# A transformer layer on eight cores: residual loads moved to ScalarE's queue, the cast cut in quarters, the output projection started 14 steps earlier

## The reference

```python
# attention: x [sq*b, 2048], 16 heads of 128
mixed = x @ Wqkv.T                       # q, k, v of each head
attn = softmax(einsum('gqd,gkd->gqk', q, k) / sqrt(128))
ctx = einsum('gqk,gkd->gqd', attn, v)
out = ctx @ Wproj.T + bproj
h1 = layernorm(x + out)
# FFN: weights are 4-bit codes times a scale per group of 128
gate, up = split(h1 @ w_gu.T)            # 5632 each
y = (silu(gate) * up) @ w_down.T
y = y / sqrt(mean(y*y) + 1e-6)
return layernorm(h1 + y)
```

## Time and profile before

| what | us |
|---|---|
| median of 3 runs | 4144.91 |
| the profiled execution, its own time | 4153.74 |
| its span, slowest core (core 2) | 4152.0 |
| spans of the eight cores | 4127.6 to 4152.0 |
| busy: PE | 4060.1 (98%) |
| busy: ACT | 1400.2 (34%) |
| busy: DVE | 948.6 (23%) |
| busy: POOL | 286.4 (7%) |

### The profile page before, as it was taken

How to read it: one execution, slowest core, us unless ns; L and a number is a source line. 1 busy time by engine, 2 the same in 40 slices (tenths; PEclk the granted TensorE clock), 3 DMA queues, 4 the chain that set the end, 5 groups by cost and what they waited for, 6 DMA issues and landing times.

```text
span 4152.0 us, 66120 instructions; the slowest of 8 cores (4127.6 to 4152.0 us)
## 1 busy us (share of the span) xinstructions
PE 4060.1 (98%) x26491; PEld 2296.5 (55%) x26881; DVE 948.6 (23%) x1433; ACT 1400.2 (34%) x1610; POOL 286.4 (7%) x434
## 2 busy tenths in 40 slices
PE   7999999999999999999999999999999999999998
PEld 4666666666666766666554444444444444444443
DVE  0054452222222223220234100022100300022124
ACT  1355555555555555557642100000000000000001
POOL 1100000000000000000223000000000000000000
PEclk9999999999999999999999999999999999999999
DMA  9777776465655655656459545447444654446433
GB/s 146 130 172 169 178 165 126 107 137 121 124 119 118 140 104 120 135 119 111 110 157 261 191 167 199 159 155 231 152 157 152 201 189 152 157 164 216 162 127 123
DMA packets 251041, 635.65 MB, mean 153 GB/s; under 512 B 115184, under 2 KB 137712, under 8 KB 212720
## 3 DMA queue, kind: packets, MB, share of 16 engines
q1 hardware_dynamic: 202496, 426.29, 31.6%
q0 software_dynamic: 45792, 196.10, 25.5%
q10 hardware_dynamic: 2448, 8.91, 0.5%
HBM read 643.83 MB, written 119.54 MB: 184 GB/s over the span
## 4 chain that ended last, share of the span: by engine, by line
PE 93%; SPq 2%; DMA 2%; issue 1%; ACT 1%; DVE 0%; POOL 0%; ACTq 0%; DVEq 0%; POOLq 0%
PE pJ L283 16%; PE pC L339 11%; PE pJ L269 11%; PE pS L320 10%; PE pS L412 7%; PE pS L393 7%; PE pS L389 7%; PE pC L389 4%; PE pJ L393 3%; PE pC L393 3%; PE pJ L389 3%; PE pJ L361 3%; PE pC L412 3%; PE pJ L412 3%; SPq L1118 2%
## 5 line engine op out<-in xcount | busy, mean ns | idle before, releaser
L496 ACT ACTIVATE P<-pS 128x1024 bf16<-128x1024 f32 x1024 | 1027.8, 1026 | 356.8 <-PE pS L320 342.6
L283 PE MATMUL pJ<-x,wq 128*128 128x512 bf16 x2984 | 756.9, 381 | 28.5 <-DMA x<-xc 23.8
L339 PEld LDWEIGHTS pC<-V,P 128*128 128x128 bf16 x8192 | 549.8, 98 | 168.0 <-issue 11.3
L339 PE MATMUL pC<-V,P 128*128 128x129 bf16 x8192 | 634.0, 220 | 3.6 <-DVE ctxg L613 3.1
L320 PE MATMUL pS<-Q,K 128*128 128x512 bf16 x1829 | 561.7, 379 | 18.9 <-ACT P L496 7.5
L269 PE MATMUL pJ<-wq,x 128*128 128x256 bf16 x4096 | 514.8, 273 | 0.4
L283 PEld LDWEIGHTS pJ<-x,wq 128*128 128x128 bf16 x3072 | 301.0, 98 | 381.9 <-issue 33.4
L269 PEld LDWEIGHTS pJ<-wq,x 128*128 128x128 bf16 x4096 | 400.7, 98 | 134.8
L609 DVE RECIPROCAL rcp<-pC 128x4 f32<-128x4 f32 x64 | 11.7, 183 | 1477.9 <-PE pC L339 1477.9
L393 PE MATMUL pS<-h1T,wgu 128*128 128x512 bf16 x1408 | 318.3, 379 | 0.0
L389 PE MATMUL pS<-h1T,wgu 128*128 128x512 bf16 x1408 | 318.3, 379 | 0.0
(11 more groups left out here) (107 smaller groups left out, 2647.8 us busy)
## 6 DMA issues: line engine op xcount, KB each, us to landing
wgu<-wgu_scr SPq DMA_DIRECT2D x176, 1024.0 KB, 4.9
x<-xc POOLq DMA_DIRECT2D x256, 512.0 KB, 12.4
wd<-wdn_scr SPq DMA_DIRECT2D x174, 512.0 KB, 3.5
wgu_scr<-bits SPq DMA_DIRECT2D x44, 1024.0 KB, 5.1
wdn_scr<-bits SPq DMA_DIRECT2D x44, 512.0 KB, 4.6
xr<-xrows SPq DMA_DIRECT2D x16, 1024.0 KB, 7.1
h_scr<-h1f POOLq DMA_DIRECT2D x16, 1024.0 KB, 7.1
res<-h_scr POOLq DMA_DIRECT2D x16, 1024.0 KB, 8.9
```

The source lines that it names most:

```text
L283: mm = t.matmul(out, M.wq[:, pair, part, hc, h * 128:(h + 1) * 128], x[:, hc, :], start=(hc == 0), stop=(hc == HC - 1))
L339: mm = t.matmul(M.pC[:, o:o + 129], M.P[n % 3][:, h * 512 + qt * 128:h * 512 + (qt + 1) * 128], M.V[s % 2][:, 2 * p + h, l, :], start=(p = ...
L496: a.activation(out=M.P[n % 3][:], in_=M.pS[n % 2][:], func=AF.Exp, bias=0.0, scale=NORM).then_inc(S.exp_done, 1)
```

## The change

Four things are changed.

1. `OC_FIRST` goes from 60 to 46: the output projection's matmuls begin at step 46 of slot 7.
2. The loads of `xr` for tiles 2 to 15 leave SP's queue. ACT issues them, each right behind the store of the `h1b` tile two before it. The first two stay on SP.
3. The cast of a tile to bf16 is cut into four instructions of 512 columns. In slot 7 one quarter stands behind each exponential; in the tail the four stand together. Every quarter waits for `h1_done` of the tile.
4. In the FFN, the four transposed loads of the next chunk stand behind operations 8, 15, 22 and 29 of the current chunk, one each. The first four context loads are placed at step 31 instead of 34, behind the same store.

```diff
-OC_FIRST = 60
+OC_FIRST = 46
+H1T_OPS = (8, 15, 22, 29)
...
-def act_h1_cast(a, S, M, tile):
+def act_h1_cast(a, S, M, k):
+    tile, ut = divmod(k, 4)
+    cols = slice(512 * ut, 512 * (ut + 1))
     a.wait_ge(S.h1_done, tile + 1)
     if tile >= 2:
         a.wait_ge(S.h1b_stored[tile % 2], 16 * (tile // 2))
-    a.copy(out=M.h1b[tile % 2][:].rearrange("t (u j p) -> t u j p", u=4, j=4),
-           in_=M.h1f[tile % 2][:].rearrange("t (u p j) -> t u j p", u=4, j=4)
-           ).then_inc(S.h1b_done, 1)
+    cast = a.copy(out=M.h1b[tile % 2][:, cols].rearrange("t (j p) -> t j p", j=4),
+                  in_=M.h1f[tile % 2][:, cols].rearrange("t (p j) -> t j p", j=4))
+    if ut < 3:
+        return
+    cast.then_inc(S.h1b_done, 1)
     a.wait_ge(S.h1b_done, tile + 1)
     a.dma_start(out=M.d_h1b[tile * 128:(tile + 1) * 128, :],
                 in_=M.h1b[tile % 2][:]).then_inc(S.h1b_stored[tile % 2], 16)
+    if tile + 2 < TILES:
+        a.wait_ge(S.oc_evac, 4 * (tile + 1))
+        a.dma_start(out=M.xr[tile % 2][:], in_=M.d_xrows[(tile + 2) * 128:(tile + 3) * 128, :]
+                    ).then_inc(S.xr_in[tile % 2], 16)
...
-        if n >= (SLOTS - 1) * STEPS and 4 * (tile + 1) <= oc_groups_done(n % STEPS - 5):
-            act_h1_cast(a, S, M, tile)
-            tile += 1
-    while tile < TILES:
-        act_h1_cast(a, S, M, tile)
-        tile += 1
+        if n >= (SLOTS - 1) * STEPS and 4 * (k // 4 + 1) <= oc_groups_done(n % STEPS - 5):
+            act_h1_cast(a, S, M, k)
+            k += 1
+    for k in range(k, 4 * TILES):
+        act_h1_cast(a, S, M, k)
...
-        if i == 34:
+        if i == 31:
...
-        sp_xr_load(y, S, M, xr + 2)
-        xr += 1
...
-            if op == 10 and ch + 1 < FCH:
-                sp_h1t_load(y, S, M, ch + 1, range(4))
+            if op in H1T_OPS and ch + 1 < FCH:
+                tt = H1T_OPS.index(op)
+                sp_h1t_load(y, S, M, ch + 1, range(tt, tt + 1))
```

More of the change, by code:

```diff
@@ L549, in act_program @@
         g += 1
-    tile = 0
+    k = 0
     for n in range(SLOTS * STEPS):
@@ L1101, in sp_ctx_load @@
                           ).then_inc(S.ctxt_in[tile % CTXT_RING], 16)
[L1104 to L1108, removed]
 def sp_h1t_load(y, S, M, ch, tiles):
@@ L1153, in sp_program @@
     y.wait_ge(S.pv_done, (SLOTS - 1) * STEPS)
-    sp_xr_load(y, S, M, 0)
-    sp_xr_load(y, S, M, 1)
-    xr = ctxt = 0
+    for tile in range(2):
+        y.dma_start(out=M.xr[tile][:],
+                    in_=M.d_xrows[tile * 128:(tile + 1) * 128, :]).then_inc(S.xr_in[tile], 16)
+    done = ctxt = 0
     for i in range(STEPS):
@@ L1164, in sp_program @@
                 ctxt += 1
-        if 4 * (xr + 1) <= oc_groups_done(i - 2):
-            sp_xr_load(y, S, M, xr + 2)
-            xr += 1
-        while ctxt - CTXT_RING < xr and 32 * (ctxt // 4 + 1) <= i:
+        if 4 * (done + 1) <= oc_groups_done(i - 2):
+            done += 1
+        while ctxt - CTXT_RING < done and 32 * (ctxt // 4 + 1) <= i:
             sp_ctx_load(y, S, M, ctxt)
@@ L1173, in sp_program @@
         y.wait_ge(S.ctx_stored[j], 16 * (SLOTS * QBLOCKS // 2))
-    while xr + 2 < TILES:
-        if xr == TILES - 5:
+    for tile in range(done, TILES - 2):
+        if tile == TILES - 5:
             sp_wgu_load(y, S, M, 0)
             sp_wgu_load(y, S, M, 1)
-        if xr >= TILES - 4:
-            sp_h1t_load(y, S, M, 0, range(2 * (xr - TILES + 4), 2 * (xr - TILES + 4) + 2))
-        while ctxt < TILES and ctxt - CTXT_RING <= xr:
+        if tile >= TILES - 4:
+            tt = 2 * (tile - TILES + 4)
+            sp_h1t_load(y, S, M, 0, range(tt, tt + 2))
+        while ctxt < TILES and ctxt - CTXT_RING <= tile:
             sp_ctx_load(y, S, M, ctxt)
             ctxt += 1
-        sp_xr_load(y, S, M, xr + 2)
-        xr += 1
     sp_wgu_load(y, S, M, 2)
```

## The result

The changed kernel is slower. Its time is 4181.70 and 4183.79 us, against 4142 to 4147 before; the ratio is 1.0092, 95% interval 1.0062 to 1.0121. Runs in which the cores of a die showed a lower granted clock (two here, 4637 and 4725 us, and one of the kernel before) are left out of every time and ratio. I had forecast 4166, with 4148 to 4190.

What follows compares the result with a forecast made beforehand. PE, busy 98% of the span, was taken as the bound. Core 0: 4139.4 + 13.4 + 2.7 - 5 + 21 - 7.4 = 4164, plus 1.7 us outside the span: 4166, range 4148 to 4190.

Steps and rivals of the forecast that it cites:

- The loop through ACT, the load, POOL and DVE: Projection's tail: each `h1f` waits on the previous one through cast, store, residual load, bias and deviation; 18.3 us a lap.
- L: Time for a residual load issued by ACT to land; taken as 6.5 us, between rows of 5.3 and 9.7.
- The tail's start: Zero point of the tail's sum, read as 2139.83 before the change, with the last exponential ending five us ahead.
- The crowding of the last two loads: Tail's end: four transposed `h1T` loads on SP run beside the last two residual loads, adding 2 us each.
- The waits and the clock: Tail: PE waits for the addition at eight tiles, 3 to 6 us each.
- The early start: Projection from step 46: a gain of 1.7 us alone, 2.7 us waiting for the first context; about +1 together.
- The quarters: Cast cut in four: 4.1 us for four in a row; PE's waits beside the exponentials shrink, -5 us.
- The spread `h1T` loads: FFN: PE's weight waits and slow matmuls behind them go, 18 us on core 2 and 7.4 on core 0.
- the loads land on time: Rival for the tail: the loop does not bind, 19 us less there on core 0, time 4126; 7%.
- a light loop: Rival for the tail: L 5.3, lap 17.1, nothing added at the end, time 4151; 15%.
- a heavy loop: Rival for the tail: L 9.7 at each lap, tail 197, time 4190; 15%.
- The spreading does nothing: Rival for the FFN: spreading the `h1T` loads gains nothing, time 4173, inside the forecast's own range; no separate chance given.

Runs made afterwards that it cites:

- experiment 1: Changed kernel with the residual loads of tiles 2 to 15 issued by SP again, where they stood before: 4127.91 us, ratio 0.9963 to the kernel before.
- experiment 2: Changed kernel with POOL adding the bias to only 64 of the 2048 columns: 4148.80 us, ratio 0.999 to the kernel before.
- experiment 3: Changed kernel with ACT issuing the residual load ahead of the cast's four quarters, not behind their store: 4143.98 us, ratio 1.0005 to the kernel before.
- experiment 4: Changed kernel with the first chunk's four `h1T` loads one at a tile, not together: 4161.90 us, ratio 1.0045 to the kernel before.
- experiment 6: Changed kernel with the projection from step 60 again: 4179.19 and 4187.26 us; with residual loads on SP as well: 4131.41 us, ratio 0.9958.
- experiment 9: Changed kernel, residual loads on SP, `h1T` one a tile: residual ahead of context load, from step 50, 4151.45 us; transposes first, weights one a tile, 4132.21 us.

## Why the prediction was right, point by point

- **The loop through ACT, the load, POOL and DVE**: right, in mechanism and in size. I had 18.3 us a lap, of which L 6.5; plain laps of core 7 are 17.3 to 19.0 and L was 6.3 in the lap shown, 5.5 to 7.1 in the others. The 6.5 was a choice between 5.3 and 9.7, so that it came this near is in part luck. Experiments 1, 2 and 3 each take away another link, and each time the lap falls to PE's pace or near it. By the estimate from the Trainium skill ("DMA: Bandwidth & Descriptors", "Anatomy of one DMA — SWDGE (gpsimd) path"), whose fit is for DMAs that GpSimd issues, the load would have taken 5.6 us; 6.3 was measured in that lap.
- **The tail's start**: I read 2139.83 as its beginning. That row was cut at the edge of the window asked for; the stretch began at 2138.11. The last exponential ends 3.3 us before the tail, not 5.0, and the tail before was 157 us, not 155.6. On core 2 the error of 1.7 us falls out of the comparison, since it moves both ends. On core 0 I worked the tail out as 151.7 us; the trace has 154.5 (2138.34 to 2292.85), because the 160 matmuls behind the wait of 3.99 us took 37.40 us and not 34.5. So its +21 should have been about +20.
- **The crowding of the last two loads**: the right cause, wrongly placed and wrongly sized, and the miss of the sum. I put 2 us on each of the last two loads, those of tiles 14 and 15. These landed in 5.5 and 6.0 us on core 7. The four transposes stand behind the last context load and met the load of tile 13, which took 26.2 us. That one lap took 38.0 us instead of 18.3; on core 1, with the same program, it took 20.0, the lap before it 20.2, and its span is 4150.9. The slowest core sets the time, so the term is worth some 15 to 20 us, not 4. With it 4166 becomes about 4182. Spreading those four loads (experiment 4) took 20 us off.
- **The waits and the clock**: I had eight waits of 3 to 6 us. On core 7 there are nine, of which four are 3.3 to 4.9, one is 3.8 at the last group, three are 1.0 to 1.8 and one is 22.3. The lap is as forecast, but I had left the clock out, which moves time from the waits into the matmuls. At the end of the tail nothing hides it: the last 32 matmuls, behind a wait of 3.80 us, took 9.85 us, where 0.216 each makes 6.9.
- **The early start**: first context tile awaited 2.8 us on core 7 and 0 to 4.1 on the others, forecast 2.7; the value 0 within what can be measured (experiment 6), forecast +1.
- **The quarters**: four in a row take 4.13 to 4.17 us, forecast 4.1; PE's waits for P fell by 5.8 us, forecast 5. The rule in the Trainium skill ("ScalarE: Activation LUTs", "Rules for kernel authors": about 0.3 us for every ACTIVATE), as I had applied it, would have given 4.8 us. It is stated for an ACTIVATE with its bias as a pointer operand, which the casts do not have; here three further instructions added 0.08 us each over the whole cast's 3.90.
- **The spread `h1T` loads**: right. Core 2's 13.5 us are gone, and the same wait is gone on the other cores; core 3 alone has a new one of 3.7 us for weights at the FFN's start.
- **The rivals**: "the loads land on time" and "a light loop" fell, and "a heavy loop" fell as put, since L was not long at every lap; a single load was four times as long. "The spreading does nothing" fell too: the waits went.

## What to carry to other kernels

When an issue moves to another engine's queue, write down what it stands behind there and follow the chain until it meets itself: here a load that waited for nothing came to wait for the cast of the previous result, and a loop of 18 us closed around 13.8 us of matmuls. A lap that is longer than the bound engine's work costs its excess at every turn, however small the parts; moving the issue ahead of the cast, or back, cures it. And look at what transposed loads stand beside: four together made one lap twice as long, one at a tile did not (experiment 4), and of the two versions of experiment 9 the one with the transposes ahead of the plain transfers was 0.3% faster, though its weights stood elsewhere too.

## What the runs showed of the hardware that was not expected

- With transposed loads and plain transfers in flight together the DMA engines moved 72 and 90 GB/s at DMA shares of 1.40 and 1.23, where a plain lap moved 175 at 0.55. Landings rose from 6 to 26 us for a megabyte, and to 27 and 36 us for transposed loads. It did not happen on every core of the same run (38.0 us against 20.0 for the same lap), and what tips it was not settled.
- A wait of PE can cost more than its own length: behind one of 4.24 us the next 64 matmuls took 16.92 us and not 13.97. And the granted clock can stay down without further waits: 0.81 for 150 us on two cores in experiment 2. What holds it there is open.
- A DMA issued by ACT behind a store half its size landed no later than one on SP's queue: 6.2 us as the median of 14, against 7.1 before.
